# Attention: the mask's product in 64-row tiles, heads interleaved over the partitions with fewer transfers, and query, key and value projections in three split terms

## What is computed

```
x = x + attention(x)        # 16 heads of 16 features; this is where the change is
x = x + traces(x)           # leaky sums over time, gates, a normalisation
x = x + experts(x)          # 256 -> 1024 -> 256, a part of it by batch element
x = x + attend(x, keys)     # softmax attention to a given tensor
```

```
lam = 10 * exp(-5 * u_prev);  use_sparse = lam >= 1
Q, K, V = (x @ W.T + b, in 16 heads)
dense_out  = softmax(Q K^T / 4 + lam * bias) V       # bias: 0 or -1 by a mask
sparse_out = softmax(Q K[idx]^T / 4, masked) V[idx]  # 32 keys by index for each query
out = where(use_sparse, sparse_out, dense_out) @ Wo.T + bo
```

## Time and profile before

| | before |
|---|---|
| median of 3 runs (2028.49 to 2030.67) | 2030.63 us |
| the profiled execution's own time | 2027.18 us |
| its span, from the first to the last instruction | 2025.2 us |
| TensorE busy over the span | 1897.5 us (94%) |
| VectorE busy | 1491.4 us (74%) |
| ScalarE busy | 1189.4 us (59%) |
| GpSimd busy | 699.3 us (35%) |
| mean granted clock of TensorE, share of 2.4 GHz | 0.968 |

### The profile page before, as it was taken

One profiled execution on the slowest core, in us unless ns is written; L12 is line 12 of the kernel. 1 busy time (PEld: TensorE's weight loads), 2 busy tenths in 40 slices (PEclk: granted clock), 3 DMA queues, 4 the chain that ended last, 5 costly groups with the idle time before them and its releaser, 6 DMA issues. The chain is left out here.

```text
span 2025.2 us, 42780 instructions
## 1 busy us (share of the span) xinstructions
PE 1897.5 (94%) x14030; PEld 1434.2 (71%) x14030; DVE 1491.4 (74%) x2206; ACT 1189.4 (59%) x2458; POOL 699.3 (35%) x719
## 2 busy tenths in 40 slices
PE   6999999999999998289999999999949999999998
PEld 4455555555555554178888888888849999999997
DVE  6788888878888887387878778778736666666664
ACT  1566666666666665246666666666644555555553
POOL 3244444544444444343343433433301111111111
PEclk8899999999999998599999999999969999999998
DMA  4455655655555553100000000000012222222231
GB/s 81 92 110 111 111 108 105 108 101 110 108 110 111 106 106 65 39 1 1 0 0 0 0 0 0 0 0 0 0 52 74 77 87 70 75 88 70 71 92 45
DMA packets 108700, 125.76 MB, mean 62 GB/s; under 512 B 31216, under 2 KB 73200, under 8 KB 108656
## 3 DMA queue, kind: packets, MB, share of 16 engines
q1 hardware_dynamic: 92272, 102.09, 24.3%
q0 software_dynamic: 15360, 22.58, 4.3%
q10 hardware_dynamic: 1024, 0.53, 0.1%
HBM read 56.41 MB, written 9.44 MB: 33 GB/s over the span
## 5 line engine op out<-in xcount | busy, mean ns | idle before, releaser
L394 DVE TENSOR_REDUCE a_top<-a_s 128x4 f32<-128x1024 f32 x256 | 310.1, 1212 | 129.0 <-PE a_s L631 128.6
L494 ACT ACTIVATE a_e<-a_t 128x512 f32<-128x512 f32 x512 | 277.7, 596 | 133.6 <-PE a_t L645 131.7
L404 DVE SCALAR_TENSOR_TENSOR a_e<-a_e,a_w_t 128x1024 f32<-128x1024 f32 x256 | 331.1, 1294 | 6.1 <-ACT a_e L494 6.1
L1717 ACT ACTIVATE c_hid<-c_pH,c_b 128x256 f32<-128x256 f32 x256 | 107.4, 471 | 187.9 <-PE c_pH L1780 187.4
L910 POOL TENSOR_TENSOR b_decayed<-b_table,b_mod_t 128x1024 f32<-128x1024 f32 x64 | 118.8, 1876 | 210.8 <-ACT b_mod_t L1182 203.5
L1341 PE MATMUL b_pS<-b_gated_t,b_decayed 128*128 128x256 f32 x768 | 183.8, 390 | 1.0
L627 PE MATMUL a_s<-a_add_m,ident_bf 128*128 128x512 bf16 x512 | 159.0, 393 | 10.4 <-POOL a_add_m L229 5.5
L660 PE MATMUL a_v<-a_e,a_v_pad 128*32 128x256 f32 x2048 | 165.2, 395 | 1.8 <-ACT a_raw L515 1.1
L1780 PE MATMUL c_pH<-c_x_hi,c_w_hi 128*128 128x256 f32 x512 | 150.3, 294 | 12.4 <-DVE c_w_lo L1682 12.2
L1341 PEld LDWEIGHTS b_pS<-b_gated_t,b_decayed 128*128 128x128 f32 x768 | 142.7, 192 | 23.5 <-issue 6.6
L631 PEld LDWEIGHTS a_s<-a_st 48*128 48x128 f32 x1024 | 78.3, 189 | 112.3 <-issue 112.3
(11 more groups left out here) (253 smaller groups left out, 5194.2 us busy)
## 6 DMA issues: line engine op xcount, KB each, us to landing
a_st<-a_split SPq DMA_DIRECT2D x768, 64.0 KB, 2.5
a_xs<-in_xT SPq DMA_DIRECT2D x32, 256.0 KB, 2.8
x_all<-in_xT SPq DMA_DIRECT2D x32, 256.0 KB, 2.8
a_r_rep<-a_r_rows POOLq DMA_DIRECT2D x32, 256.0 KB, 5.1
c_we<-in_we SPq DMA_DIRECT2D x32, 256.0 KB, 2.7
c_key_t<-in_keyT SPq DMA_DIRECT2D x32, 256.0 KB, 3.2
c_value<-in_key SPq DMA_DIRECT2D x32, 256.0 KB, 2.7
out<-c_y POOLq DMA_DIRECT2D x32, 256.0 KB, 3.2
```

The costliest lines, as they stand in the source:

```text
L394: dve.tensor_reduce(top[:, qc, half].rearrange("p (r j c) -> p r j c", r=2, j=2)[:, :, cc], ps_s[g % 2][:], AX.X, ALU.max)\
L404: dve.scalar_tensor_tensor(out=buf[:], in0=buf[:], scalar=BIG, in1=w_t[par][:, kc].unsqueeze(1).to_broadcast([P, 4, S]), op0=ALU.min, op1= ...
L494: act.activation(e[g % E_BUFS][:, 2 * r:2 * r + 2], ps_t[r][:], ACT.Exp).then_inc(exp_done, 1)
L1717: ins = act.activation(hid[r % 2][:, i], pH[r][:, i], ACT.Gelu, bias=b1[:, 2 * r + i:2 * r + i + 1])
```

## The change

It has four parts, in the attention layer and in how the host lays out its weights.

1. The mask's product runs in the two row tiles of 64 rows. `absent2` holds the mask in bf16, each half of the queries in both halves of the partitions; `eye` is a selection matrix times the element's sparse flag, made by GpSimd from `halves` (128 x 256 instead of 128 x 512). Four matmuls of 64 rows and 512 columns take the place of two of 128 rows.
2. Heads are interleaved: head j has partitions j, j+4, ..., and the three terms stand at every fourth row of the stack. One transfer fills both row tiles, so that a batch element has 12 stack transfers of 128 KB instead of 24 of 64 KB; the maxima's row is one transfer from SP instead of two from ScalarE, `merge` one instead of four, `spread` two instead of one. The row tiles use 63 and 64 rows instead of 48 and 49.
3. The query, key and value projections are done in three terms of float32r: 12 matmuls of one pass. The weights are split once in the setup. The input is split for each element: `high_xs` on ScalarE, `low_xs` on GpSimd; the input tile `xs` is single, its split parts are double.
4. Places in the order: `turn_max` behind `score_cols`; `project_q` behind `mix_values` in group 0; `project_v` in groups 2 and 3; `residual` and the reciprocal one group later.

```diff
             sp.wait_ge(stack_free[half], n + 1)
             for done, count, term, first, step in ((hi_done, n + 1, 0, 1, 1), (lo_done, 2 * n + 1, 1, 1, 2), (lo_done, 2 * n + 2, 2, 0, 2)):
                 sp.wait_ge(done, count)
-                for r in range(2):
-                    for j in (2 * half, 2 * half + 1):
-                        rows = split[par][64 * r + 16 * j:64 * r + 16 * j + 16, first:first + step + 1:step].bitcast(F32)
-                        sp.dma_start(st[par][64 * r + 16 * term:64 * r + 16 * term + 16, :, j].bitcast(F32), rows)\
-                          .then_inc(d_stack[half][par], 16)
-
+                for j in (2 * half, 2 * half + 1):
+                    sp.dma_start(st[par][term::4, :, j].bitcast(F32), split[par][j::4, first:first + step + 1:step].bitcast(F32))\
+                      .then_inc(d_stack[half][par], 16)
+
+        def place_max(n, par, half):
+
+            sp.wait_ge(mrow_done[half], n + 1)
+            sp.dma_start(st[par][63::64, 0, 2 * half:2 * half + 2].bitcast(F32), max_row[half][:].bitcast(F32)).then_inc(d_max[half], 16)
+
+        def staged(n):
+
+            sp.wait_ge(xs_lo_done, n)
+            sp.dma_start(xs[:], t["xT"][bass.ds(n, 1)].rearrange("o (k p) s -> p (o k) s", p=P)
+                         if not isinstance(n, int) else t["xT"][n].rearrange("(k p) s -> p k s", p=P)).then_inc(d_xs, 16)
...
         def body(n, par, stage, proj, maxi):
             if maxi:
                 stack(n + 1, 1 - par, 1)
+            place_max(n, par, 1)
             at_least(sp, d_x, n * 16)
             sp.dma_start(X[:, :, bass.ds(n * S, S)] if not isinstance(n, int) else X[:, :, n * S:n * S + S],
                          t["xT"][bass.ds(n, 1)].rearrange("o (k p) s -> p (o k) s", p=P)
                          if not isinstance(n, int) else t["xT"][n].rearrange("(k p) s -> p k s", p=P)).then_inc(d_x, 16)
+            if stage:
+                staged(n + 3)
             if proj:
                 stack(n + 2, par, 0)
-            if stage:
-                staged(n + 3, 1 - par)
-
-        staged(2, 0)
+            if maxi:
+                place_max(n + 1, 1 - par, 0)
...
-            pool.tensor_tensor(add_m[par][:], absent[:], mix_n[par][:, 0:1].unsqueeze(2).to_broadcast([P, C, S]), ALU.mult)\
+            pool.tensor_tensor(eye[par][:], halves[:], mix_n[par][:, 0:1].unsqueeze(2).to_broadcast([P, 2, P]), ALU.mult)\
                 .then_inc(m_ready, 1)
...
-            for j in range(4):
-                pool.dma_start(raw_v[par][0][32 * j + 16:32 * j + 32], raw_v[par][1][32 * j + 16:32 * j + 32]).then_inc(d_merge, 16)
+            pool.dma_start(raw_v[par][0][1::2], raw_v[par][1][1::2]).then_inc(d_merge, 16)
...
-            pool.dma_start(r_rep[:].rearrange("p c s -> p (c s)"),
-                           r_rows.rearrange("j h s -> (j h) s").unsqueeze(1).to_broadcast([8, DH, C * S])).then_inc(d_rep, 16)
+            for half in range(2):
+                pool.dma_start(r_rep[half::2].rearrange("p c s -> p (c s)"),
+                               r_rows[:, half].unsqueeze(1).to_broadcast([4, DH, C * S])).then_inc(d_rep, 16)
...
+        def low_weight(i, low, w, high):
+
+            pool.wait_ge(scaled, 3 + i)
+            pool.tensor_tensor(low[:], w[:], high[:].bitcast(F32), ALU.subtract).then_inc(w_lo_done, 1)
+
+        def low_xs(n, par):
+
+            pool.wait_ge(xs_hi_done, n + 1)
+            pool.tensor_tensor(xs_lo[par][:], xs[:], xs_hi[par][:].bitcast(F32), ALU.subtract).then_inc(xs_lo_done, 1)
...
+            if stage:
+                after_weigh(n, 6)
+                low_xs(n + 3, 1 - par)
             if not (isinstance(n, int) and n < 3):
-                after_weigh(n, 6)
+                after_weigh(n, 7)
                 residual(n - 3)
             if finish:
...
+        def high_xs(n, par):
+            act.wait_ge(d_xs, 16 * (n + 1))
+            if not (isinstance(n, int) and n < 2):
+                act.wait_ge(proj_v, n - 1)
+            act.activation(xs_hi[par][:], xs[:], ACT.Copy).then_inc(xs_hi_done, 1)
...
+        def place_absent():
+
+            act.wait_ge(set_up, ABSENT)
+            for hq in range(2):
+                for r in range(2):
+                    act.dma_start(absent2[64 * r:64 * r + 64, :, hq], absent[64 * hq:64 * hq + 64]).then_inc(d_absent, 16)
...
         def project_q(n, par):
-            pe.wait_ge(d_xs[par], landed(n, par))
+            pe.wait_ge(xs_lo_done, n + 1)
             if isinstance(n, int) and n < 2:
                 at_least(pe, v_done, n)
             else:
                 pe.wait_ge(mrow_done[1], n - 1)
+            product(n, par, wq_lo, wq_hi).then_inc(proj_q, 1)
+
+        def product(n, par, w_lo, w_hi):
+
+            terms = [(a, b, k) for k in range(C) for a, b in ((w_hi, xs_hi[par]), (w_lo, xs_hi[par]), (w_hi, xs_lo[par]))]
             for m in range(C):
-                for k in range(C):
-                    ins = pe.matmul(bank[:, m], wq[:, k, m * P:m * P + P], xs[par][:, k], start=(k == 0), stop=(k == C - 1))
-            ins.then_inc(proj_q, 1)
+                for i, (a, b, k) in enumerate(terms):
+                    ins = pe.matmul(bank[:, m], a[:, k, m * P:m * P + P], b[:, k], start=(i == 0), stop=(i == len(terms) - 1))
+            return ins
...
-            for m in range(C):
-                for k in range(C):
-                    ins = pe.matmul(bank[:, m], wk[:, k, m * P:m * P + P], xs[par][:, k], start=(k == 0), stop=(k == C - 1))
-            ins.then_inc(proj_k, 1)
+            product(n, par, wk_lo, wk_hi).then_inc(proj_k, 1)
...
-            for k in range(C):
-                ins = pe.matmul(bank[:, m], xs[par][:, k, m * P:m * P + P], wv[:, k], start=(k == 0), stop=(k == C - 1))
+            terms = [(a, b, k) for k in range(C) for a, b in ((xs_hi[par], wv_hi), (xs_hi[par], wv_lo), (xs_lo[par], wv_hi))]
+            for i, (a, b, k) in enumerate(terms):
+                ins = pe.matmul(bank[:, m], a[:, k, m * P:m * P + P], b[:, k], start=(i == 0), stop=(i == len(terms) - 1))
...
-            for r in range(2):
-                pe.matmul(ps_s[g % 2][:, r], ident_bf[:], add_m[par][:, qc].unsqueeze(1).to_broadcast([P, C, S]), start=True, stop=False)
+            for hq in range(2):
+                for r in range(2):
+                    rows = slice(64 * r, 64 * r + 64)
+                    pe.matmul(ps_s[g % 2][:, r], eye[par][rows, hq], absent2[rows, qc, hq].unsqueeze(1).to_broadcast([64, C, S]),
+                              start=(hq == 0), stop=False, tile_position=(64 * r, 0))
             for c in range(C):
                 for r in range(2):
-                    rows = slice(64 * r, 64 * r + 48)
+                    rows = slice(64 * r, 64 * r + 63)
                     ins = pe.matmul(ps_s[g % 2][:, r, c], st[par][rows, 0, j, c, qc * P:qc * P + P], st[par][rows, 1, j, c],
                                     start=False, stop=(c == C - 1), tile_position=(64 * r, 0))
...
+        def body(n, par, stage, proj, maxi, finish):
             for g in range(GROUPS):
                 if maxi:
                     score_rows(n + 1, 1 - par, g)
+                score_cols(n, par, g)
                 if g == 0:
                     turn_max(n, 1)
                 if g == 5 and maxi:
                     turn_max(n + 1, 0)
-                score_cols(n, par, g)
-                if g == 0 and proj:
-                    project_q(n + 2, par)
                 if g == 1 and proj:
                     project_k(n + 2, par)
-                if maxi and g in (3, 4):
-                    project_v(n + 1, 1 - par, g - 3)
+                if maxi and g in (2, 3):
+                    project_v(n + 1, 1 - par, g - 2)
                 if g in (6, 7) and not (isinstance(n, int) and n < 2):
                     project_out(n - 2, par, g - 6)
                 if g > 1:
                     mix_values(n, par, g - 2)
                 elif finish:
...
-        pe.wait_ge(d_const, 16 * (len(CONSTS) + 1))
+                if g == 0 and proj:
```

166 lines of the change are left out of this document (95 added, 71 removed).

## The result

The changed kernel takes 2096.85 us, the median of 4 runs from 2093.12 to 2098.45. The kernel before took 2029.98 on the same chip (2028.49 to 2030.67). The ratio is 1.0324, 95% interval 1.0306 to 1.0341: slower, where the prediction said 2005 and faster. The profiled execution has a span of 2091.4 us.

The account below looks back on a forecast made before the run. TensorE was taken to bound the attention layer. Bodies -28, setup +4 and boundary stalls -1.5 gave -25.5 from 2027.18, 2001.7; 2005 as the median of runs, range 1972 to 2036 us.

Parts of the forecast that it names:

- Other queues, at nothing: SP, GpSimd and ScalarE queues in attention: added work is covered, costs nothing; without cover a body grows .6 to 1.4 us.
- if its clock falls there: Sign of a wrong forecast: TensorE's clock falls at a body's start, where it might wait for the maxima's row.
- SP's queue: Rival at body boundaries: maxima's row lands late behind stack transfers at half of them, 2042 us; .12 with other late transfers.
- Mask: Mask matmuls on TensorE: row tiles gain .03 us a group, .24 a body, bounds 0 and .9.
- the mask's run of .51: Mask's four row-tile matmuls on TensorE: claimed to take .51 us, bounds .43 and .55, against .54 before.
- Projections: Query, key and value projections on TensorE: twelve one-pass matmuls gain .99 us a body, bounds .9 and 1.1.
- the wait for the row of maxima: TensorE's wait before the query run: moving that run behind the value product removes it, .20 us a body.
- VectorE's answer: VectorE in each attention body: nearly as long as TensorE, so waits return .5 us, bounds .2 and 1.2.
- the walk: Groups 2 to 7 followed in time: product of group 5 waits 0 or .1 us for VectorE, group 6 .3.
- Setup and ends: Setup before the first mask: splits add 4 us, bounds 1 and 8, first mask at 43 us.
- Switches are what costs: Rival on TensorE's array layout changes: .18 us each, 34 become 24 a body; body 21.65, total 1976 us; chance .17.
- the forecast of 22.67: Attention body after the change: 22.67 us, .93 less than before, including .5 of waits for VectorE.

Follow-up runs that it names:

- experiment 1: Changed kernel with the residual put back to wait for 6 weightings, ahead of the new subtraction on GpSimd: 1980.73 us, ratio .9761.
- experiment 3: Changed kernel with two buffers for delta, ScalarE's copy of the output projection, residual left where the change put it: 1969.39 us, ratio .9703.
- experiment 4: Kernel before the change, with one edit: the residual waits for 7 weightings instead of 6: 2132.67 us, ratio 1.0515.
- experiment 6: Kernel of experiment 3 with the mask's product back on the full array, the mask made by GpSimd for each element: 1995.68 us, ratio .9839.
- experiment 7: Kernel of experiment 3 with query, key and value projections back in float32, no splits, two input buffers: 1983.91 us, ratio .9773.
- experiment 11: Kernel of experiment 3 with the query's projection back ahead of group 0's value products: 1976.69 us, ratio .9734.
- experiment 8: Kernel of experiment 3 with each stack transfer cut in two, 24 of 64 KB, partitions still spread: 1971.74 us, ratio .9712.
- experiment 2: Changed kernel with the residual waiting for 6 weightings again, but still behind the new subtraction on GpSimd: 2051.92 us, ratio 1.0112.
- experiment 9: Kernel of experiment 3 with the residual back behind group 6's weighting, ahead of the split of x: 1980.98 us, ratio .9746.

## Why the prediction was wrong

**The step that failed** is "Other queues, at nothing". It costed GpSimd's new subtraction by how busy the engine is ("its 332.84 of 720 leave room") and allowed a body "that instruction, .6 to 1.4 us" if the cover were gone. It never costed the residual's move by a group and behind that subtraction, though the change shows it. GpSimd had room, and was not late for want of it: it was idle for 1.27 us before the addition, which starts .2 us behind the weighting that it waits for. What counts is when its end lets ScalarE's copy start, and who stands behind the copy. From the end of the seventh weighting at 405.8 the addition (1.26 us) and the copy (.84) take until 408.15, and TensorE has been idle for 2.87 us by 408.19. Experiments 1, 3 and 4 show it from three sides: the residual put back, the buffer, and the later weighting alone on the kernel before. Of the prediction's own signs of being wrong, one came, "if its clock falls there", though behind another wait than the one it thought of.

**The size.** From experiment 3 to the changed kernel the body grows from 21.49 to 25.44, 3.95 us. Over the 28.3 bodies of 60 to 780 us the wait is 73.3 us, 2.6 a body. The clock, 1.00 in experiment 3 and .92 in the changed kernel in the windows from 100 to 700 us, would be .08 x 25.44 = 2.0 a body if all work took twice as long at .50. It does not. The same instructions, from the transposes to the key's first matmul, take 6.21 us behind the gap (408.19 to 414.40) and 3.93 in experiment 3, .18 of it waiting:

```profile
403.88 0.38 PE L740 MATMUL a_bank<-ident,a_top 128*8 128x128 f32 x2
...
407.81 0.39 PE L641 MATMUL a_bank<-a_xs_hi,a_wk_hi 128*128 128x256 f32 x1
```

That is 2.46 lost where half of 6.21 is 3.1, so I estimate the clock at 2.0 x .79 = 1.6 a body. Together that is 4.2, .25 more than the growth. Some of the surplus is that the clock is low already in the gap, where it costs nothing (.92 in the gap shown).

The rival "SP's queue" had the right picture, a gap at the boundary with a slow query run behind it, but in half of the bodies, on another queue, and at 2042; in the stretch TensorE waited for the row's transfer once (1.3 us).

**Mask.** Predicted .03 a group with bounds 0 and .11; measured .19 on TensorE (experiment 6). The mis-sized term is the mask's run of .51. It was composed as if each run's overhead came on top of its streaming. In the trace the mask hands over to the scores after .25 and the scores take .43 in place of .34, together .68, in which the scores start while the mask's row (.60) still runs. I read this as a row tile going on with scores while the other still streams; the rows do not show the tiles apart. The prediction let the further weight loads eat part of the gain; .04 us is all that is left of overhead in eight matmuls. The Trainium skill (TensorE: Matmul & The Clock Gate, Packing small matmuls) states that a weight load overlaps running matmuls only where its row group differs. The mask's matmuls alternate between the two row tiles, so each load can find the other one's matmul running, and the .04 does not speak against that rule; the prediction's reading of it does not hold. The Trainium skill (TensorEngine Tiling (Array Packing), Key Properties) also states that a change of tiling mode drains the engine. That fits the .19, though no run here parts the drain from the weight loads.

**Projections.** Predicted .99, and .20 for the wait for the row of maxima. On TensorE experiment 3 has the query run at 1.63 (405.01 to 406.64), the key at 1.62 and a value half at .90: .27, .30 and .32 for both halves less, .89 and not .99. Experiment 7 gives .66 in the body; the waits for VectorE's weighting are 15.3 us in 650 there and 21.6 in experiment 3, which is the other .2. The query's place was worth .29 (experiment 11).

**VectorE's answer.** Predicted .5 (.2 to 1.2); experiment 3 has 21.6 us of waits for the weighting in 650, .7 a body. They fall in groups 5 and 6, as walked through, with .33 and .23 where the walk had .1 and .3, and in the body above in group 0 too (.18), where the walk had none:

```profile
418.38 0.64 PE L721 MATMUL a_v<-a_e,a_v_pad 128*32 128x256 f32 x8 [0.33 <-DVE a_e L447]
...
421.33 0.64 PE L721 MATMUL a_v<-a_e,a_v_pad 128*32 128x256 f32 x8 [0.23 <-DVE a_e L447]
```

**Setup and ends.** Predicted +4 up to a first mask at 43 us. The first mask stands at 47.08 in the changed kernel and at 42.4 to 46.9 in the experiments with the same setup. Before it TensorE waits 4.83 us for the copy of the absence mask, a transfer that the sum left out; but before the change it waited 5.45 at the same place for GpSimd's mask, and without that copy, in experiment 6, the first mask stands at 43.85. So what the transfer adds stays open. Not foreseen at all: 7 to 8 us more between the last body and the next layer (experiment 3: 50.4 against 42.6), 5.2 of them behind the last residual. I have not tried what they are.

**The rest of the sum.** With the chain cured, the change gains 2.20 us a body: 23.69 to 21.49. Undone one at a time, the row tiles give .88, the split projections .66, the query's place .29, the transposes' place 0. That leaves .37 open. The effects need not add up, since VectorE's waits absorb a part of each: counted on TensorE they are 8 x .19, .89 and .29, less the .7 of waits for VectorE that came, 2.0 in all. The last .2 stays open; the earlier groups of the value projection were not tried. The rival "Switches are what costs", a body of 21.65 and 1976 us, comes within 7 us of this kernel; the forecast of 22.67 does not. That is in part luck: it gave the layout changes 1.8 a body, where the mask gave 1.5, and it had +4 for the setup and nothing for the end, which came to 4.7 and 7.8 in this run.

## What to carry to other kernels

When an instruction moves on a queue, follow its end, not its engine's load: list who waits for it, through which buffer, and whether the engine that sets the time stands behind that. A one-buffer tile between three engines (written by one, read by another, with the writer holding a bank that a third needs) is a chain that a move of one group can bring into the open, at the price of the gap and of the slower clock behind it. The kernel before had .15 us to spare, and no wait of TensorE showed it. A second buffer took it out here, and was worth nothing as long as the chain was early.

## What the runs showed of the hardware

**Transfers.** The stack transfers move the same bytes, but the DMA engines are busy for much less time. The page's queue rows for 100 to 750 us, of the kernel before, of experiment 3 (12 transfers a body) and of experiment 8 (24):

```profile
q1 hardware_dynamic: 46508, 57.55, 48.7%
```

```profile
q1 hardware_dynamic: 43454, 60.28, 26.7%
```

```profile
q1 hardware_dynamic: 48875, 60.23, 27.1%
```

The kernel before wrote 16 partitions side by side, both later ones every fourth partition: the share nearly halves with the spread, and the number changes nothing. No run undoes the spread alone; between the kernel before and experiment 8 it is what differs in these transfers. One of 64 KB landed after 2.5 us, and lands after 2.0 with the spread; one of 128 KB takes 2.1. It brought no time here, since TensorE hardly waited for these transfers.

**The clock.** It does not follow the length of a gap. Between 60 and 780 us it fell to .50, the lower level of 1.2 GHz, behind each of the 23 gaps of experiment 4, nearly all of 2.0 and 2.3 us; behind 13 of the 26 of experiment 2, nearly all of 2.5; and behind 24 of the 25 of the changed kernel, nearly all of 2.9 and 3.05. A gap of 1.58 in the kernel before had a slow query run behind it too. So the cost of a gap is its length and up to 2.5 us more, and the length alone does not say which.

**GpSimd under VectorE.** Between 100 and 740 us of the changed kernel and of experiments 1, 2, 3 and 9, 78 of the residual's additions and the splits of x start while a weighting (L447) runs on VectorE. Each of them takes 2.18 to 2.29 us. The other 188 take 1.26 to 1.29, also where a weighting starts while they run. The traces show this and not the reason; to a chain it is worth as much as a place in the queue.
